# Chain set-up taken in steps 0 and 1, a reordered opening, passage and last steps, and one VectorE reciprocal for both inverse variances

## The reference

```python
x = x + attn_a(layernorm(x))     # linear attention: q,k = elu(..)+1, kv = k^T v, out = q kv / (q sum k)
x = x + ffn(layernorm(x))        # relu(x Ws1)^2 Ws2; routed experts have probability trunc(softmax), 0 but for a tie
x = x + attn_b(layernorm(x))     # iterated attention (3 rounds) over the first 16 tokens of each batch;
                                 # every other token gets only the bias ob
x = x + ffn(layernorm(x))
```

## Time and profile before

| | before |
|---|---|
| device time, median of 3 runs | 451.77 us (450.33 to 453.6) |
| the profiled execution's own time | 452.05 us |
| span of that execution | 450.3 us |
| PE busy | 419.2 us (93%) |
| PE weight loads | 345.3 us (77%) |
| DVE busy | 321.0 us (71%) |
| ACT busy | 218.2 us (48%) |
| POOL busy | 251.1 us (56%) |

### The profile page before, as it was taken

How to read it: one execution, slowest core, us unless ns; L and a number is a source line. 1 busy time by engine, 2 the same in 40 slices (tenths; PEclk the granted TensorE clock), 3 DMA queues, 4 the chain that set the end, 5 groups by cost and what they waited for, 6 DMA issues and landing times.

```text
span 450.3 us, 7753 instructions
## 1 busy us (share of the span) xinstructions
PE 419.2 (93%) x2570; PEld 345.3 (77%) x2570; DVE 321.0 (71%) x687; ACT 218.2 (48%) x385; POOL 251.1 (56%) x350
## 2 busy tenths in 40 slices
PE   8998999999999998798889999999999999999971
PEld 4777889879888997677667876787887887878740
DVE  4779976577667747478637897977777876987842
ACT  2766687777776773233243442243333423434430
POOL 3576776676677742135426357564627537544462
PEclk9999999999999999999999999999999999999997
DMA  8701211111100003001010111011011011011111
GB/s 258 220 19 43 87 55 47 48 47 47 47 0 1 0 1 96 3 1 52 3 48 2 52 48 49 4 49 48 2 48 45 6 49 48 18 33 49 49 48 57
DMA packets 22776, 20.59 MB, mean 46 GB/s; under 512 B 3254, under 2 KB 22716, under 8 KB 22716
## 3 DMA queue, kind: packets, MB, share of 16 engines
q1 hardware_dynamic: 22156, 19.32, 13.5%
q10 hardware_dynamic: 560, 0.52, 0.4%
HBM read 11.32 MB, written 8.45 MB: 44 GB/s over the span
## 4 chain that ended last, share of the span: by engine, by line
PE 61%; DVE 11%; ACT 11%; POOL 8%; issue 6%; POOLq 1%; DMA 1%; DVEq 0%; ACTq 0%
PE PB L1421 6%; PE PT L1460 6%; PE PA L1421 5%; PE PB L1442 5%; PE PA L1490 4%; PE PA L1496 3%; PE PA L1491 3%; PE PT L1500 3%; ACT scratch L567 3%; PE PA L1432 3%; POOL ln_rstd L436 3%; PE PG L1296 2%; ACT o_hi L750 2%; POOL ln_rstd L434 2%; DVE ln_bn L788 2%
## 5 line engine op out<-in xcount | busy, mean ns | idle before, releaser
L486 POOL TENSOR_TENSOR ln_a<-ln_bn 128x4 f32<-128x4 f32 x32 | 6.5, 203 | 120.7 <-DVE ln_bn L991 120.7
L458 POOL TENSOR_TENSOR xn_pair<-scratch,xn_pair 128x1024 fp32r<-128x1024 f32 x16 | 38.4, 2400 | 18.9 <-ACT xn_pair L578 18.9
L871 DVE SCALAR_TENSOR_TENSOR scratch<-scratch,PB 128x512 f32<-128x512 f32 x32 | 20.9, 683 | 36.5 <-ACT scratch L611 36.3
L991 DVE BATCH_NORM_STATS2 ln_bn<-x_all 128x6 f32<-128x256 f32 x128 | 44.9, 413 | 0.9
L567 ACT ACTIVATE scratch<-x_all,ln_shift,ln_rstd 128x255 f32 (+1 forms) x60 | 31.1, 591 | 22.6 <-POOL ln_shift L440 22.6
L743 ACT ACTIVATE scratch<-PA,ln_rsq 128x256 f32<-128x256 f32 x32 | 13.4, 470 | 59.1 <-PE PA L1421 35.3
L447 POOL TENSOR_TENSOR x_all<-x_all,wvo 128x1024 f32 (+1 forms) x16 | 38.6, 2410 | 0.1
L447 POOL TENSOR_TENSOR x_all<-x_all,ob_rows 128x1024 f32<-128x1024 f32 x16 | 37.7, 2358 | 0.0
L1269 PE MATMUL PB<-wk_hi,xt_hi 128*128 128x256 f32 x128 | 36.9, 288 | 0.6 <-DVE xt_lo L816 0.4
L1490 PE MATMUL PA<-wo_hi,o_hi 128*128 128x256 f32 x128 | 33.6, 295 | 3.1 <-ACT o_hi L750 2.7
L1271 PE MATMUL PB<-wk_hi,xt_lo 128*128 128x256 f32 x128 | 36.2, 283 | 0.0
(11 more groups left out here) (246 smaller groups left out, 1167.4 us busy)
## 6 DMA issues: line engine op xcount, KB each, us to landing
out_dram<-x_all SPq DMA_DIRECT2D x16, 512.0 KB, 3.2
x_all<-n_L_attn_a_inputs_q_dram SPq DMA_DIRECT2D x15, 512.0 KB, 3.5
x_all<-n_L_attn_a_inputs_q_dram ACTq DMA_DIRECT2D x2, 128.0 KB, 3.0
x_all<-n_L_attn_a_inputs_q_dram SPq DMA_DIRECT2D x2, 128.0 KB, 2.8
setup<-in_L_attn_a_Wk_dram SPq DMA_DIRECT2D x1, 256.0 KB, 5.3
setup<-in_L_attn_a_Wq_dram ACTq DMA_DIRECT2D x1, 256.0 KB, 5.5
wvo<-in_L_attn_a_Wv_dram SPq DMA_DIRECT2D x1, 256.0 KB, 7.0
wvo<-in_L_attn_a_Wo_dram SPq DMA_DIRECT2D x1, 256.0 KB, 6.0
```

The source lines that it names most:

```text
L458: nc.gpsimd.tensor_tensor(xn_pair[:, :, 1, :], xn[g % 2], xn_pair[:, :, 0, :].bitcast(F32), ALU.subtract).then_inc(x_lo, 1)
L991: nc.vector.bn_stats(ln_bn[:, slot, t:t + 1, :], x_tile(n, t)).then_inc(bn, 1)
```

## The change

- **Opening.** ACT runs one tiny activation as soon as a constant stands, before its first real work. The first group's tiles 0 to 2 are normalised on DVE and only tile 3 on ACT (before: two and two). PE transposes each tile as it comes, and no longer waits for the bias rows before the first six passes of the fold.
- **Passage and step 0.** PE makes the transposes of G first, then `fold_ffn`; the transposes OT stand ahead of `fold_ffn_product`, whose result goes to PT. DVE makes `w1c` before `batch_kv`.
- **Chain set-up.** The vectors, block matrices and bias rows get a place of their own in a tensor that lies over weights of pass 1, so the vectors are loaded right after the last q product, ahead of the big weights. DVE's blocks move from (2,1) to (0,1), PE's products from (2,2), (2,3), (3,1), (4,1) to (0,2), (0,3), (1,1), (1,3), ACT's copies from (2,2), (2,3), (3,1), (3,2), (4,2) to (0,2), (0,3), (0,3), (1,2), (1,3).
- **Inverse variances.** POOL keeps the five small operations; the power is gone. One DVE reciprocal of up to 8 elements takes both slots, behind the norm's reciprocal and ahead of L1010.
- **wo.** The hi products go by feature half c first, and each half waits for its own half of o_hi.
- **Last steps.** At step 16 PE's product into PA (L1421) stands behind f1 and r2, with ACT's and DVE's scaling behind their own work for f1. At step 17 DVE scales all four tiles, ACT and POOL none, and SP stores in two halves.

The core of the diff, SP:

```diff
-                if runs(v):
+                if v == NG - 1:
+                    for h in range(2):
+                        sp.wait_ge(out_dve, 2 * NG + 2 * h)
+                        sp.dma_start(out_dram[nv, :, 2 * h:2 * h + 2, :], x_all[:, nv * T + 2 * h:nv * T + 2 * h + 2, :]).then_inc(stored, 16)
+                elif runs(v):
...
             sp.wait_ge(q_mm, C * NG)
-            for dst, w in zip(raw4, (qw, kw, vw, ow)):
-                sp.dma_start(dst, rows(w)).then_inc(c_wts, 16)
-            sp.wait_ge(o_mm, 1)
             for dst, w in zip(l_rows, (lqw, lkw, lvw)):
...
+            for dst, w in zip(raw4, (qw, kw, vw, ow)):
+                sp.dma_start(dst, rows(w)).then_inc(c_wts, 16)
```

POOL:

```diff
-            def rsq(slot, j, bn, powed, done):
...
+            def four_variances(slot, j, bn, done):
...
-                pool.wait_ge(powed, 5 * j + 5)
-                nc.gpsimd.tensor_tensor(ln_rsq[:, slot, :], a, minus_ones[:, :], ALU.pow).then_inc(done, 1)
+                nc.gpsimd.tensor_tensor(a, both[:, :, 2], both[:, :, 5], ALU.add).then_inc(done, 1)
...
+                nc.gpsimd.tensor_tensor(a, a, d, ALU.add).then_inc(done, 1)
...
+                ge(pool, rsq, i - 1)
                 if runs(r):
-                    ge(pool, r2_mm, r)
-                    rsq(0, r, bn2, pow2, rsq2)
+                    four_variances(0, r, bn2, var2)
                 if runs(v):
-                    ge(pool, out_dve, 2 * v)
-                    ge(pool, f4_scaled, 2 * v)
-                    rsq(1, v, bn3, pow3, rsq3)
+                    four_variances(1, v, bn3, var3)
...
-                if runs(v):
+                if runs(v) and v < NG - 1:
```

ACT:

```diff
+            act.wait_ge(setup_dve, 1)
+            nc.scalar.activation(ln_rsq[:, 1, 0:1], minus_one[:, 0:1], ACT.Identity, scale=minus_one[:, 0:1],
+                                 bias=minus_one[:, 0:1]).then_inc(table_ready, 1)
             act.wait_ge(rstd1, 1)
-            for t in range(2, T):
-                nc.scalar.activation(xn[0][:, t:t + 1, 0:D - 1], x_tile(0, t)[:, :, 0:D - 1], ACT.Identity, scale=ln_rstd[:, 0, t:t + 1],
-                                     bias=ln_shift[:, 0, t:t + 1]).then_inc(norm1, 2)
+            t = T - 1
+            nc.scalar.activation(xn[0][:, t:t + 1, 0:D - 1], x_tile(0, t)[:, :, 0:D - 1], ACT.Identity, scale=ln_rstd[:, 0, t:t + 1],
+                                 bias=ln_shift[:, 0, t:t + 1]).then_inc(norm1, T)
             act.wait_ge(folded, 1)
...
-                if (i, slot) == (2, 2):
+                if (i, slot) == (0, 2):
...
-                elif (i, slot) == (2, 3):
+                elif (i, slot) == (0, 3):
                     act.wait_ge(c_brow, 1)
-                    act.wait_ge(o_mm, 4)
                     nc.scalar.activation(bias_all, PG[0:SP, 1, :], ACT.Copy).then_inc(c_taken, 1)
-                elif (i, slot) == (3, 1):
...
-                elif (i, slot) == (3, 2):
+                elif (i, slot) == (1, 2):
...
-                elif (i, slot) == (4, 2):
+                elif (i, slot) == (1, 3):
...
+                if runs(v) and i < NG:
+                    scale_tiles(i, v)
...
+                if i == 0:
+                    fold_ffn_product()
...
+                if i == NG:
+                    scale_tiles(i, v)
```

DVE:

```diff
+            def reciprocal_variances(i, r, v):
+
+                slots = slice(0 if runs(r) else 1, 2 if runs(v) else 1)
+                if runs(r):
+                    dve.wait_ge(var2, 5 * (r + 1))
+                    ge(dve, r2_mm, r)
+                if runs(v):
+                    dve.wait_ge(var3, 5 * (v + 1))
+                    ge(dve, f4_scaled, 2 * v)
+                nc.vector.reciprocal(ln_rsq[:, slots, :], ln_a[:, slots, :]).then_inc(rsq, 1)
+
+            def scaled_sum(i, v, nv):
+
+                dve.wait_ge(f4_mm, v + 1)
+                dve.wait_ge(rsq, i)
+                if v < B:
+                    dve.wait_ge(c_xs, 16 * (v + 1))
+                for t in range(2 if v < NG - 1 else T):
+                    nc.vector.scalar_tensor_tensor(x_tile(nv, t), four(PA)[:, t:t + 1, :], ln_rsq[:, 1, t:t + 1], x_tile(nv, t),
+                                                   ALU.mult, ALU.add).then_inc(out_dve, 1)
...
                     nc.vector.reciprocal(norm_inv[:, :, :], norm_sb[:, :, :]).then_inc(o_norm, 1)
+                    if runs(r):
+                        reciprocal_variances(i, r, v)
                     dve.wait_ge(o_norm, 2 * i + 2)
...
+                else:
+                    reciprocal_variances(i, r, v)
                 if i == 0:
-                    batch_kv(B - 1)
                     dve.wait_ge(fold_sb, 1)
...
+                    batch_kv(B - 1)
+                if runs(v) and i != NG:
+                    scaled_sum(i, v, nv)
...
+                if i == NG:
+                    scaled_sum(i, v, nv)
...
-                if at == (2, 1):
+                if at == (0, 1):
...
+                elif at == (2, 1):
```

PE:

```diff
+            pe.wait_ge(w_loaded, 16)
+            fold_weight(PA, wk_raw)
             pe.wait_ge(bias_ready, 2)
-            pe.wait_ge(w_loaded, 16)
-            fold_last_row(PA, wk_raw, bk_rows)
-            pe.wait_ge(norm1_dve, 2)
+            fold_bias(PA, bk_rows)
...
             for t in range(T):
-                if t >= 2:
-                    pe.wait_ge(norm1, 2 * (t - 1))
+                if t < T - 1:
+                    pe.wait_ge(norm1_dve, t + 1)
+                else:
+                    pe.wait_ge(norm1, T)
                 for c in range(C):
                     last = nc.tensor.transpose(PT[:, c, t * P:(t + 1) * P], xn[0][:, t, c * P:(c + 1) * P], ident[:, :])
...
+                    g_transposes(B - 1)
                     fold_ffn()
-                    g_transposes(B - 1)
                     kv_product(B - 1)
...
+                if runs(v) and i != NG:
...
-                if i == 0:
-                    fold_ffn_product()
                 if runs(i):
                     pe.wait_ge(o_done, 3 * (i + 1))
...
+                if i == 0:
+                    fold_ffn_product()
...
+                if i == NG:
+                    pe.wait_ge(f3_sq, v + 1)
+                    pe.wait_ge(t2_done, C * NG)
+                    down(PA, h3, f4_mm)
...
-                    pe.wait_ge(o_hi_done, C * (i + 1))
...
                     for tiles in ((0, 2), (1, 3)):
-                        for t in tiles:
-                            for c in range(C):
+                        for c in range(C):
+                            pe.wait_ge(o_hi_done, C * i + c + 1)
+                            for t in tiles:
...
-                if at == (2, 2):
+                if at == (0, 2):
...
-                elif at == (2, 3):
+                elif at == (0, 3):
...
-                elif at == (3, 1):
+                elif at == (1, 1):
...
-                elif at == (4, 1):
+                elif at == (1, 3):
```

102 lines of the change are left out of this document (51 added, 51 removed).

## The result

The changed kernel took 434.24 us (median of 4 runs, 433.9 to 434.56) against 452.23 for the kernel before beside it: ratio 0.9598, 95% interval 0.9571 to 0.9625. I had forecast 438.3, at the least 435.0. The profiled execution took 434.53 us, span 432.7.

The account below looks back on a forecast made before the run. PE was taken to bound the kernel, busy 173.0 of 174.3 us in steps 5 to 15. Gains of 0.8 + 9.5 - 0.5 + 3.7 = 13.5 us gave 438.55, or 438.3 against the median, range 435 to 443.

Parts of the forecast that it names:

- Opening, -0.8: Start of the kernel: moving ACT's table load and one tile to DVE brings 0.8 us, bounds 0 and 1.3.
- group 1 comes only 0.8 earlier: Opening: group 1's statistics stand behind the Wq part on DVE, so it gains only 0.8 us and PE waits for it.
- Passage and step 0, -0.75: From the passage to T2 of step 1: 0.75 us gained, T2 at 187.45 against 188.18 before the opening's gain.
- Five threads: Passage and step 0: vectors, blocks on DVE, PE, wo to T2, and ACT's bias rows meet; together 0.75 us gained.
- Steps 1 to 4, T2 of step 5 at 242.85: The chain's 2.8 us and most PE waits leave steps 1 to 4; passage to step 4 gains 9.5 us.
- Shared reciprocal and halves, steps 5 to 15, +0.5: Steps 5 to 15: the reciprocal's new waits outweigh the gain of wo by halves, costing 0.5 us, bounds -1 and +4.
- The halves' -1.1: Steps 5 to 15: wo by halves gives back about 0.3 us in each of three steps, 1.1 in all.
- The reciprocal's +1.6: Steps 5 to 15: the shared reciprocal's new wait makes division, OT and o_lo late, priced at 1.6 us.
- Its first part: Steps 8, 11 and 13: division and OT late behind slot 1's variance, 0.25 us in step 11, 0.6 for the three.
- Its second part: Steps 5, 10 and 12: o_lo 0.2 to 0.45 us late behind the chain's work on DVE, +1.0.
- My rival by this rule: Steps 5, 10, 12, 15: chain's SBUF work loses DVE/POOL port lock, 1.2 us each, +1.6 overall, 439.9 us; chance 0.08.
- Last steps, -3.7: Steps 16 and 17: moved product, DVE scaling and half stores gain 3.7 us, bounds 2.5 and 4.3.

Follow-up runs that it names:

- late_table: The changed kernel without ACT's early operation, so its table load stands again behind the first standard deviations: 435.11 us against 434.24.
- rows_first: The changed kernel with DVE's blocks waiting for their own three loads instead of all twelve: 432.94 us against 434.24.
- old_places: The changed kernel with the chain set-up's operations back at steps 2 to 4, loads and tiles kept: 435.88 us against 434.24.
- one_store: The changed kernel with the last group stored by one 512 KB transfer instead of two of 256 KB: 435.03 us against 434.24.

## Why the prediction was wrong, and where it was right

**Opening, -0.8: right in kind, 0.35 too small.** What the table load counts, 0.5 to 1.24, hangs on POOL (late_table), which the prediction did not ask. The mis-sized step is "group 1 comes only 0.8 earlier": its transposes came 1.14 earlier, like the k product, and with it the whole first part. The 0.35 is no larger than what varies anyway: in the ten other kernels with after's opening intact group 1 came between 18.43 and 19.14 (18.77 in after), which is 0.8 to 1.5 before the 19.91 of before.

**Passage and step 0, -0.75 (with the opening, T2 of step 1 at 186.65): 186.86.** The total hides that this term nearly vanished: with 1.14 from the opening in the 1.32, passage and step 0 gave 0.18, not 0.75. Five threads met much as said. The mis-sized term is the vectors: the last landed 9.5 after the first issue (170.54 to about 180.0), not 8.75, so PE waited 1.14 for the blocks, not 0.6, and that is the loss.

```profile
170.54 0.81 SPq L388 DMA_DIRECT2D ffn_weights<-in_L_attn_b_lqw_dram  x1
...
180.06 0.70 DVE L1143 TENSOR_TENSOR ffn_weights<-ffn_weights,head_mask 128x128 f32<-128x128 f32 x3 [1.23 <-DMA ffn_weights<-in_L_attn_b_lnd_w_dram]
...
181.01 0.71 PE L1571 MATMUL PG<-ffn_weights 128*128 128x128 f32 x4 [1.14 <-DVE ffn_weights L1147]
```

The blocks at 0.28 each (0.70 for three, overlapped) were right. What I had not asked is whether DVE must wait for all twelve loads; rows_first says no.

**Steps 1 to 4, T2 of step 5 at 242.85: 242.18.** The stretch took 55.32 where the prediction had 56.2, 0.9 better than said: no wait of PE at all was left. That the time of T2 of step 5 is right within 0.7 is in part luck, since the 0.57 lost in step 0 hid more than half of this. old_places adds what the sum could not tell: the buffers, the early loads, the halves and the reciprocal together did most of it, the new places 1.3.

**Shared reciprocal and halves, steps 5 to 15, +0.5: -2.0. This is the step that failed**, and it made 2.5 of the 4 us; -2.0 lies even outside the bounds that I gave this term (-1 to +4). The halves' -1.1 was right for the kernel before (1.04). The reciprocal's +1.6 had the wrong sign. Its first part, OT late by 0.6 in steps 8, 11 and 13 together (0.25 in step 11), came to 0, 0.06 and 0.06: the reciprocal's 0.20 overlaps with the division, which starts 0.12 behind it, and the last small operation stood 5.23 behind T2 in step 11 instead of 5.32. Its second part, o_lo late in steps 5, 10 and 12, was reversed in steps 5 and 10, which are 0.73 and 0.32 shorter than with the powers. I had the contention in hand, with the earlier trace rows, and took it that sums which run a microsecond earlier hold the chain's work "about as long as before". I had not laid the sums of one step beside the operations of DVE in it. Its opening sentence on this stretch, "Nothing that another engine gains there can shorten the run", fell as well: PE's idle time of 1.3 us there looked like the most that could be won, and 2.0 was, since waits also cost overlap (the last point of this document). The powers, which PE never waited for, had pushed the large sum by 1.2 us onto DVE's operations of the chain.

The Trainium skill ("SBUF — State Buffer", Who interferes with whom) says that a DVE instruction with two SBUF inputs contends with a GpSimd instruction that reads SBUF, while one with at most one SBUF input outside the two-port modes does not. The traces agree: 1706 ns against 406 for two SBUF inputs, 0.28 us unchanged beside POOL's sum where one is in PSUM. A tensor_scalar of 128x8 took 1.0 us against 0.22; in which mode it ran no trace shows. My rival by this rule forecast 439.9; it had the rule right and the direction wrong.

**Last steps, -3.7: -4.63.** The third product of step 16 came 1.71 earlier relative to T2 (predicted 1.8), held by the reciprocal as said:

```profile
418.43 0.20 POOL L498 TENSOR_TENSOR ln_a<-ln_a,ln_d 128x4 f32<-128x4 f32 x1
...
418.82 0.20 DVE L1014 RECIPROCAL ln_rsq<-ln_a 128x8 f32<-128x8 f32 x1 [1.47 <-POOL ln_a L498]
...
419.08 0.65 PE L1517 MATMUL PT<-ident,ln_rsq 128*128 128x128 f32 x4 [1.07 <-DVE ln_rsq L1014]
...
421.30 1.02 PE L1548 MATMUL PT<-h2s,ffn_weights 128*128 128x512 f32 x2
...
428.40 1.66 DVE L1023 SCALAR_TENSOR_TENSOR x_all<-PA,ln_rsq,x_all 128x256 f32<-128x256 f32 x4
429.30 1.19 SPq L371 DMA_DIRECT2D out_dram<-x_all  x2
```

From there to the second store's issue, the last 0.4 of this pair's 1.19, it is 1.6 less than in the earlier trace rows (predicted 1.4). The half store is the mis-sized term: 0.5 predicted, 1.34 measured, 0.71 of it shown by one_store.

Together: 0.35 opening, 0.3 up to step 5, 2.5 in the long stretch and 0.9 at the end make the 4.1 us by which the sum missed, counted in the span. All four sums erred the same way; a result below 436 had a chance of 0.05, and no rival of mine described it.
